# Attention and a mixture of experts on one core: the order behind the last attention unit, the experts' first bias as a row of the weights, a second raw buffer, and fewer waits between the adds

## The reference

```python
x = x + tanh(g_xattn[0]) * xattn(layernorm(x), ctx, ctx, Wq, bq, Wk, bk, Wv, bv, Wo, bo)
x = x + tanh(g_ffn[0]) * ffn(layernorm(x), ...)

# ffn
hs = einsum('bsd,ndf->nbsf', x, sw1) + sb1            # shared expert
shared_out = einsum('nbsf,nfd->bsd', swiglu(hs), sw2) + sb2.sum(0)
probs = softmax(x @ gate_w + gate_b)
topk_probs, topk_idx = top_k(probs, 2)
cw = sum(one_hot(topk_idx, 8) * topk_probs[..., None], axis=2)
hr = einsum('bsd,edf->ebsf', x, rw1) + rb1            # first product and first bias
out_e = einsum('ebsf,efd->ebsd', swiglu(hr), rw2) + rb2
return shared_out + einsum('ebsd,bse->bsd', out_e, cw)
```

## Time and profile before

| | us |
|---|---|
| median of 3 runs | 694.46 |
| lowest and highest run | 694.03 and 696.72 |
| the profiled execution | 697.65 |
| its span, first to last instruction | 695.8 |
| PE busy / DVE / ACT / POOL, of the span | 635.5 / 482.7 / 424.3 / 230.7 |

### The profile page before, as it was taken

The page is one execution under the profiler, slowest core; times in us unless marked ns, Lnnn a source line. Parts: engine busy times, 40 slices in busy tenths (PEclk is TensorE's granted clock), DMA queues, the critical chain, the costliest instruction groups (busy, mean ns, idle before and its releaser), DMA issues.

```text
span 695.8 us, 12724 instructions
## 1 busy us (share of the span) xinstructions
PE 635.5 (91%) x3603; PEld 332.6 (48%) x3616; DVE 482.7 (69%) x805; ACT 424.3 (61%) x842; POOL 230.7 (33%) x243
## 2 busy tenths in 40 slices
PE   3997687999999999999999999999988989999990
PEld 3776561223333333333333333345456778888870
DVE  4785879778888888888888888847777844444430
ACT  4674344777777777777777777766734224444440
POOL 2343324303431442244100211220057804555552
PEclk9998897999999999999999999999999999999995
DMA  7999697964697689767843660224079665655445
GB/s 238 333 270 310 222 233 176 154 97 95 143 192 197 187 157 186 193 172 153 163 62 61 90 106 32 92 75 168 24 266 312 231 184 87 102 98 96 73 47 143
DMA packets 82820, 108.22 MB, mean 156 GB/s; under 512 B 16553, under 2 KB 64563, under 8 KB 81814
## 3 DMA queue, kind: packets, MB, share of 16 engines
q1 hardware_dynamic: 71912, 78.58, 49.0%
q0 software_dynamic: 10864, 29.10, 15.8%
HBM read 62.10 MB, written 47.35 MB: 157 GB/s over the span
## 4 chain that ended last, share of the span: by engine, by line
PE 65%; issue 13%; POOL 6%; DVE 6%; DMA 5%; SPq 2%; ACT 1%; POOLq 1%; ACTq 0%; DVEq 0%
PE psS L1492 16%; PE psO L1519 16%; PE psM L1474 14%; PE psH L1737 8%; PE psY L1763 3%; POOL zs L720 3%; DMA kq<-k_parts 2%; DVE mneg L1125 1%; PE psO L1416 1%; DVE mneg L1049 1%; PE psX L1725 1%; PE psH L1748 1%; DMA acc<-ysb,ids 1%; PE psF L1446 1%; POOL parts L614 1%
## 5 line engine op out<-in xcount | busy, mean ns | idle before, releaser
L1125 DVE TENSOR_REDUCE mneg<-psM 128x1 f32<-128x1024 f32 x240 | 282.6, 1219 | 60.7 <-PE psM L1474 60.7
L859 ACT ACTIVATE pr<-psS 128x512 f32<-128x512 f32 x488 | 266.7, 595 | 94.8 <-PE psS L1492 94.8
L1492 PE MATMUL psS<-kq 99*128 99x512 bf16 x488 | 152.4, 385 | 2.1 <-DMA kq<-msb 1.5
L1519 PE MATMUL psO<-pr,vt 128*32 128x512 f32 x1024 | 136.4, 605 | 0.0
L1474 PE MATMUL psM<-kq 96*128 96x512 bf16 x480 | 127.3, 386 | 4.8 <-DVE mneg L1125 3.1
L1492 PEld LDWEIGHTS psS<-kq 99*128 99x128 bf16 x488 | 39.8, 97 | 149.6 <-ACT pr L859 131.3
L766 POOL DMA_INDIRECT acc<-ysb,ids x39 | 60.2, 1543 | 66.9 <-ACT ysb L982 32.1
L600 POOL TENSOR_TENSOR msb<-mcp,none 16x128 bf16<-16x128 f32 x16 | 6.2, 389 | 224.7 <-ACT mcp L836 224.7
L1474 PEld LDWEIGHTS psM<-kq 96*128 96x128 bf16 x480 | 46.2, 98 | 63.4 <-DVE mneg L1125 9.1
L1737 PE MATMUL psH<-wall,zgT 128*128 x234 | 68.2, 427 | 0.9 <-DVE zgT L1357 0.9
L1363 DVE TENSOR_TENSOR rg<-psH,rs 128x256 f32<-128x256 f32 x39 | 16.5, 424 | 66.4 <-ACT rs L970 66.4
(11 more groups left out here) (246 smaller groups left out, 828.5 us busy)
## 6 DMA issues: line engine op xcount, KB each, us to landing
kq<-k_parts SPq DMA_DIRECT2D x96, 128.0 KB, 5.7
...
v_pad<-vst SPq DMA_DIRECT2D x16, 512.0 KB, 8.7
vt<-v_pad SPq DMA_DIRECT2D x16, 512.0 KB, 7.9
...
```

Of the source, the lines that this page charges most:

```text
L859: nc.scalar.activation(pr[:, slot, j], score_bank(s, j), ACT.Exp, scale=SCALE).then_inc(e_done, 1)
L1125: V.tensor_reduce(mneg[:, parity, i:i + 1], psM[:, i % 2], X_AXIS, ALU.max, negate=True).then_inc(m_free, 1)
L1492: mm(score_bank(s, j), kst[:, slot, j, kt * P:(kt + 1) * P], qst[:, slot, j], start=True, stop=True).then_inc(s_full, 1)
L1519: last = mm(psO[j * VW:(j + 1) * VW, u % 2], vt[:, u, k, j * VW:(j + 1) * VW], pr[:, k % 4, j], start=(k == 0), stop=(k == KT - 1), skip_g ...
```

## The change

1. The first bias of the routed experts is no longer a product of its own. Of W1's 256 rows the last is subtracted from all others, and its own place takes the bias (`less_last_row`, POOL, once per expert: one DMA of the bias row, two subtractions of 128x512; `last_row_in` fetches the last row, repeated over 128 partitions). The rows that are scattered get 1.0 in their last column (a small memset in each `scatter`). `brow1`, its blanking and its loads go.
2. Raw weights lie in two buffers by turns (`wraw[:, 0]` and `raw2`), and `raw_in` is issued right behind the two writes of the expert before. `blank_rows`, the blanking of `fill` and the write of the spare rows of `acc`, moves from between `scatter(1)` and `scatter(2)` into attention.
3. An add waits only for the adds of earlier experts; the ring has 24 buffers, and ACT's wait for a free one changes accordingly.
4. Behind attention: the last unit's output is turned before the logits and the turn of batch 2 and the rankings of batches 1 and 2, which leave the tables and are written out behind the unit. `first` can be issued in halves, `r_attn(3)` writes to another bank, and the written-out orders of PE, DVE and ACT change.

```diff
-YB = 12
-DRAIN = 6
-LAST_DRAIN = 30
+YB = 24
+RUN = NQ * NB // P
...
-        b1_p = sb("b1_p", [NE * 4, 3, P], BF16, sP)
-        brow1 = sb("brow1", [P, NE, 2 * D], BF16, sZ)
+        sb("raw_shift", [P, QT * D], F32, sR)
+        raw2 = sb("raw2", [P, WCOLS], F32, sR)
...
+            sp.wait_ge(bt_ok, 1)
+            sp.dma_start(b1_rows.rearrange("e (m p) -> (e m) p", p=P), b1_t[:]).then_inc(b1_st, 16)
+            sp.wait_ge(bp_ok, 1)
             for s in range(3):
-                sp.dma_start(b1_parts[s].rearrange("(q p) -> q p", p=P), b1_p[:, s]).then_inc(bp_st, 16)
                 sp.dma_start(b2_parts[s].rearrange("(e d) -> e d", d=D), b2_p[:, s]).then_inc(bp_st, 16)
...
-            sp.wait_ge(brow_ok, 2)
-            b1_rows = b1_parts.rearrange("s (e c) -> s e c", e=NE)
-            sp.dma_start(brow1[0:3, 0:NR], b1_rows[:, 1:NE]).then_inc(brow_ld, 16)
-            sp.dma_start(brow1[0:3, NR:NE], b1_rows[:, 0:1]).then_inc(brow_ld, 16)
+            sp.wait_ge(brow_ok, 1)
             sp.dma_start(brow2[0:3], b2_parts.rearrange("s (e c) -> s e c", e=NE)).then_inc(brow_ld, 16)
             store_base(1)
...
+            def raw_at(e):
+                return raw2[:] if e % 2 else wraw[:, 0]
+            def last_row_at(nth):
+                return aT[:, nth % 2]
+            def last_row_in(nth, e):
+                nc.gpsimd.dma_start(last_row_at(nth), wexp[raw_of(e), P - 1:P, 2 * FF:4 * FF].to_broadcast([P, 2 * FF])).then_inc(last_ld, 16)
+            def less_last_row(nth, e, raw):
+                if nth == 0:
+                    pool.wait_ge(b1_st, 16)
+                nc.gpsimd.dma_start(raw[P - 1:P, 2 * FF:4 * FF], b1_rows[raw_of(e):raw_of(e) + 1]).then_inc(b1_ld, 16)
+                pool.wait_ge(last_ld, 16 * (nth + 1))
+                nc.gpsimd.tensor_tensor(raw[:, 0:2 * FF], raw[:, 0:2 * FF], last_row_at(nth), ALU.subtract).then_inc(less_ok, 1)
+                nc.gpsimd.tensor_tensor(raw[0:P - 1, 2 * FF:4 * FF], raw[0:P - 1, 2 * FF:4 * FF], last_row_at(nth)[0:P - 1],
+                                        ALU.subtract).then_inc(less_ok, 1)
+                pool.wait_ge(less_ok, 2 * nth + 2)
+                pool.wait_ge(b1_ld, 16 * (nth + 1))
...
+                raw, hi = raw_at(e), wraw[:, 1]
                 pool.wait_ge(raw_ld[0], 16 * (2 + e))
-                nc.gpsimd.tensor_copy(wraw[:, 1].bitcast(F32R), wraw[:, 0]).then_inc(wp_hi, 1)
+                less_last_row(1 + e, e, raw)
+                if e:
+                    pool.wait_ge(wp_st, 32 * e)
+                nc.gpsimd.tensor_copy(hi.bitcast(F32R), raw).then_inc(wp_hi, 1)
                 pool.wait_ge(wp_hi, e + 1)
-                nc.gpsimd.tensor_tensor(wraw[:, 0].bitcast(F32R), wraw[:, 0], wraw[:, 1], ALU.subtract).then_inc(wp_ok, 1)
+                nc.gpsimd.tensor_tensor(raw.bitcast(F32R), raw, hi, ALU.subtract).then_inc(wp_ok, 1)
                 pool.wait_ge(wp_ok, e + 1)
-                nc.gpsimd.dma_start(w_parts[e, :, 0:WCOLS], wraw[:, 1]).then_inc(wp_st, 16)
-                nc.gpsimd.dma_start(w_parts[e, :, WCOLS:2 * WCOLS], wraw[:, 0]).then_inc(wp_st, 16)
+                nc.gpsimd.dma_start(w_parts[e, :, 0:WCOLS], hi).then_inc(wp_st, 16)
+                nc.gpsimd.dma_start(w_parts[e, :, WCOLS:2 * WCOLS], raw).then_inc(wp_st, 16)
+                if e + 1 < LATE:
+                    raw_in(e + 1)
             def raw_in(e):
-                pool.wait_ge(wp_st, 32 * e)
-                nc.gpsimd.dma_start(wraw[:, 0], wexp[raw_of(e)]).then_inc(raw_ld[0], 16)
+                nc.gpsimd.dma_start(raw_at(e), wexp[raw_of(e)]).then_inc(raw_ld[0], 16)
+                last_row_in(1 + e, e)
...
+            def blank_rows():
...
+                    if n == 0:
+                        last_row_in(0, NE - 2)
+                    else:
+                        less_last_row(0, NE - 2, wraw[:, 1])
                     prepare(n, NE - 1 - n, n)
...
+                elif n == 3 + LATE:
+                    blank_rows()
...
             def scatter(b):
                 pool.wait_ge(sl_ok, b + 1)
+                nc.gpsimd.memset(zx(b)[:, :, D - 1:D], 1.0).then_inc(ones_z, 1)
+                pool.wait_ge(ones_z, b + 1)
...
-            pool.wait_ge(wp_st, 32 * LATE)
-            nc.gpsimd.memset(fill, 0.0).then_inc(fill_c, 1)
...
-            nc.gpsimd.memset(brow1[:].rearrange("p e c -> p (e c)").bitcast(F32), 0.0).then_inc(brow_ok, 1)
...
-                if i % DRAIN == 0 and i <= LAST_DRAIN:
-                    pool.wait_ge(added, 16 * (i + 1))
-                else:
-                    pool.wait_ge(added, waits[i % 4])
+                pool.wait_ge(added, waits[i % 4])
...
-                    act.wait_ge(issued, DRAIN * ((i - DRAIN) // DRAIN) + 1)
+                    act.wait_ge(issued, i - YB + RUN + 1)
...
-                                11: ((r_slots, 0), (r_choose, 1)), 12: ((r_shift, 2), (r_slots, 1))}
+                                11: ((r_slots, 0),)}
...
+            r_choose(1)
+            r_shift(2)
+            r_slots(1)
             r_choose(2)
+            r_sum(3)
+            gate(0, 0)
             r_slots(2)
-            gate(0, 0)
+            r_scale(3)
             gated_low(0, 0)
...
-                                9: ((r_logits, 1),), 10: ((r_lturn, 1), (r_turn, 2)), 11: ((r_prefix, 0), (r_logits, 2)),
-                                12: ((r_lturn, 2), (r_prefix, 1))}
+                                9: ((r_logits, 1),), 10: ((r_lturn, 1), (r_turn, 2)), 12: ((r_prefix, 0),)}
...
+            r_logits(2)
+            r_attn(3)
+            r_lturn(2)
             pe.wait_ge(w_ok, EARLY)
-            r_attn(3)
-            first(0, 0)
+            first(0, 0, (0,))
+            r_prefix(1)
+            first(0, 0, (1,))
+            r_wo(3)
             r_prefix(2)
-            r_wo(3)
             first(0, 1)
...
-                mm(psR[:, i % 2], uone[:, 1], brow1[:, bass.ds(e, 1)].rearrange("s a c -> s (a c)"), start=True, stop=False)
...
-                                  start=False, stop=(n == 2 and k == DT - 1))
+                                  start=(n == 0 and k == 0), stop=(n == 2 and k == DT - 1))
```

112 lines of the change are left out of this document (55 added, 57 removed).

## The result

| | before | after |
|---|---|---|
| median of four runs, us | 694.25 | 708.35 |
| lowest and highest | 690.95, 696.72 | 707.54, 709.59 |
| profiled execution and its span | 697.65, 695.8 | 709.59, 707.8 |

The changed kernel is **slower**: 1.0178 times the time before, 95% interval 1.0115 to 1.024. In a later series on another chip (x12) it was 1.0122 (1.0076 to 1.0167). The forecast was 681.8 us.

A forecast was written before the change was run, and what follows sets the result against it. PE was taken to bound the tiles, with three chains side by side between attention and tiles. Gains of 9.3 and 4.2 less 0.8 make 12.7 us, 694.46 to 681.8; forecast 679.5 to 684.5, range 678.8 to 687.5.

The forecast's parts named there:

- The bias product: In the tiles: without it each of 39 tiles saves 0.24 us, 9.3 us (9.1 to 9.8), all on the path.
- The adds: POOL in the tiles: the last add stays 5.2 us behind the last output, so point 3 gains nothing.
- Behind attention: Between attention and tiles: the new order starts the first tile at about 559.2 instead of 563.4, gaining 4.2 us.
- Rival 3: Behind attention: PE's clock falls, or the gain goes to a chain taken too short; 686.0 us, chance 0.12.
- Staging beside attention: POOL's staging of experts during attention: later transfers delay `load_max`, costing 0.5 us over seven units and 0.3 for the first.
- rival 2: Beside attention: staging delays `load_max` by more than 1.8 us a unit, kernel slower; 698.8 us at 2.5; chance 0.03.
- start: In the staging: the expert's write goes out some 3 us later, at about 213.6, with `load_max` at 205.26.
- work: In the staging: 18.1 us of transfers from 214.7 end at 233; `load_max` lands about 233.6, PE wants it at 234.4.
- price: Beside attention: late `load_max` costed per unit over seven units: 688.3 us at 1.0 us, 698.8 at 2.5.

The follow-up runs named there:

- x8: The kernel before with only the bias product of the tiles left out (the experts' first bias missing from the result); ratio 0.9999 to the kernel before.
- x5: Changed kernel; next raw weights and repeated row asked for between subtractions and conversion, bias row directly behind `split_max`; 685.59 us, ratio 0.9821 to the kernel before.
- x4: Changed kernel without subtracting W1's last row: no bias row, no repeated row; raw weights still behind the writes, two buffers; 682.1 us against 698.4 before.
- x1: Changed kernel; raw weights and repeated row asked for right behind `split_max`, bias row brought in with the raw weights; ratio 1.008 to the kernel before.
- d3: The kernel before; each `load_max` held back until the last product with the values, then for a small transfer of 32 KB; 817.52 us.

## Why the prediction was wrong, step by step

- **The bias product: right.** Pitch 2.64 by the starts of the six products (answer to the earlier trace rows), 9.1 us over the stretch, for 2.65 and 9.3. The forecast gave the lot to the time without a condition, though; x8 shows that it needs point 3: without it no gain is left (ratio 0.9999, interval 0.9960 to 1.0038).

```profile
604.71 1.55 PE L1773 MATMUL psH<-wall,zgT 128*128 x6
...
607.35 1.55 PE L1773 MATMUL psH<-wall,zgT 128*128 x6
```

- **The adds: number right, reason wrong.** The last add was forecast 5.2 us behind the last output and stands 5.7 (answer to the earlier trace rows). But "the dropped waits lie before the 30th tile, where POOL catches up again, so point 3 gains nothing" fails: with the faster tiles POOL does not catch up, and without point 3 6 to 7 us are lost. The sum to make was all of POOL's adds and waits against all of the tiles; I looked at one add against one tile.

```profile
689.12 0.47 ACT L1010 ACTIVATE ysb<-psY,zg 128x256 f32<-128x256 f32 x1 [0.79 <-PE psY L1799]
...
694.86 1.55 POOL L794 DMA_INDIRECT acc<-ysb,ids  x1 [0.30 <-issue]
```

- **Behind attention: right.** Against the last `split_max`, the last values came 2.8 us sooner (2.7 forecast; the first row below holds the last two groups of values in one), the output's turn 4.4 (4.7), `r_sum(3)` 4.8 (4.6), the last `slot_u` 3.0 (2.3), the first tile 4.8 (4.2). The rows of after, answers to the earlier trace rows, all 25.2 us late (the 28.3 that attention lost, less 3.1 at the start):

```profile
529.12 1.92 PE L1549 MATMUL psO<-pr,vt 128*32 128x512 f32 x16
...
533.64 1.03 PE L1609 MATMUL psH<-idn,vt 128*128 128x128 f32 x8
...
542.42 1.28 DVE L1201 SCALAR_TENSOR_TENSOR xs<-psY,tg,xs 128x1024 f32<-128x1024 f32 x1 [0.18 <-PE psY L1619]
...
565.00 0.17 DVE L1272 CAST slot_u<-slot_f 128x8 uint32<-128x8 f32 x1
...
580.65 3.10 SPq L558 DMA_DIRECT2D zg<-zs  x4
...
583.86 0.68 PE L1762 MATMUL psX<-idn,zg 128*128 128x128 f32 x4 [1.05 <-DMA zg<-zs]
```

  Rival 3 did not come: the clock of this stretch was 1.00 (answer to the earlier trace rows).

```profile
520.00:565.00 45.00, 41.69 (x256) 28.42 (x256) 34.34 (x118) 21.79 (x39) 24.26 (x31) 1.00 0.69 230
```

- **Staging beside attention: the step that failed**, +28.3 us for +0.8. It was the place of rival 2, at 0.03, whose price of 2.5 us a unit was also too low. The step fails in three terms.
  - The *start*: writes at 8.3 us past `load_max` were forecast (205.26 to 213.6); they went out 12.9 and 13.1 past it (203.43 to 216.31, 231.37 to 244.51), since a transfer stood between `split_max` and the conversion, and I had counted its issue and not its landing.
  - The *work*: 18.1 us of full engines were forecast for a unit's transfers; from the raw weights to the end of the crowd (217.4 to 238.3) it was 21. The bytes were not what was missed: before, the writes had taken 4 us and the rest, raw weights included, 13.3 (217.0 to 230.3), which with the repeated row gives the forecast's 18. I had taken the time of the engines as fixed by the bytes, and it is not. x5 moves the changed kernel's bytes and keeps the engines busy 0.81 of a unit of 23.5 us (204.48 to 227.99), 19.0 us; x4, without the repeated row but with the raw weights in the crowd, 0.94 (201.92 to 225.44), 22.1:

```profile
201.92:225.44 23.52, 23.52 (x135) 7.44 (x134) 19.44 (x19) 17.99 (x34) 8.10 (x10) 1.00 0.94 184
```

  - The *price*: a late `load_max` was costed at its wait; with the clock it costs up to 2.6 times as much (7.4 for 2.8).

  The first two add up. Against the `load_max` ahead of it the crowd starts 4.5 us later and it is 2.8 longer; the unit itself had become 4.4 longer (27.9 for 23.5), so it ends some 3 us later against the next `load_max`: 6.9 past its issue (231.37 to 238.3), where 4.2 were forecast (228.8 to 233). A late unit makes the next unit's bias row late, but not without end: behind the unit of 30.9 us the transfers had time to finish, the bias row landed in 3.0 us (262.18), the writes went out 8.4 us past `load_max`, and that unit took 23.5 without a wait.
- The Trainium skill, page "DMA: Bandwidth & Descriptors", section "Queues, rings and completion order", has each engine go round the queues with work. By it the forecast would have put the term at 3 us; the sign was right. The rows agree in this much: with 762 KB of POOL's queue beside it, `load_max`, 12 KB in all on SP's queue, took as long to land as they did (5.8 and 5.7 us in x1). In what turns the engines took, no run here shows. Its page "TensorE: Matmul & The Clock Gate", section "HAM oscillation — how this bites in real kernels", tells of a kernel whose clock falls again at every recurring wait for a DMA. The trace agrees (five slow stretches in the changed kernel, 15 in d3), and the forecast had weighed that page for turns, where nothing happened, and not for waits, where it did.
- With the staging repaired, the other steps give the forecast: x5 has the ratio 0.9821, and 681.8 over 694.46 is 0.9818. That the two agree to 0.03% is luck in part: the interval of x5 is 0.9777 to 0.9864, and the forecast counted on nothing from point 3, without which 6 to 7 us of it are lost.
